# One wait of GpSimd for four tiles' results, and the first splits ahead of the first gates

## The chip, the cores and the metric

The kernel runs on one core of a Trainium2 chip. The metric is the device time of one execution in microseconds (us). The kernel is one program in which the five engines (TensorE or PE, VectorE or DVE, ScalarE or ACT, GpSimd or POOL, SyncE or SP) each follow an instruction list of their own and are tied together by semaphores alone.

## The reference

The input x is 16 images of 128 channels of 28 x 28 positions (784 tokens of an image). Three blocks follow one another, each added to its input:

```python
x = x + conv_block(group_norm(x))                 # depthwise 3x3, relu, prune, 1x1 conv, relu, prune
t = tokens(x)                                     # 16 x 784 tokens of 128 values
t = t + spiking_attention(layer_norm(t), Wq, Wk, Wv)
flat = layer_norm(t).reshape(12544, 128)
logits = flat @ Wr                                # 8 experts
top_vals, top_idx = top_k(logits, 2); w = softmax(top_vals)
for e in range(8):                                # every token: its two experts alone have a gate
    y = gelu(flat @ W1[e] + b1[e]) @ W2[e] + b2[e]   # 128 -> 512 -> 128
    out += gate[:, e] * y
t = t + out
```

The change touches the last block only, the experts.

## The kernel before, in words

**Stages.** The first 555 us work through the images (convolution, attention, norm, routing) as a software pipeline over images, one image entering in each step. Each routed image is sent by GpSimd to a dispatch buffer in DRAM ("dispatched_rows"), sorted by expert: 14 indirect transfers of 112 rows an image (L575). Images 14 and 15 are held back, and are normed, routed and sent between the first expert tiles. Then come 105 **expert tiles** of 256 dispatched rows with one expert each, and last the **sums**: for each of the 16 images the two expert rows of each token are loaded from DRAM, added (L1561), turned by TensorE (L891), added to the residual (L1567) and stored.

**One expert tile t**, by engine:
- SyncE loads its rows turned (`xrt`, four buffers, L438) and their fields (destination, the two experts' gate arguments, L441). The fields are handled in batches of four tiles (DEEP = 4).
- TensorE: `hidden(t)`, 12 matmuls of 256 columns (four parts of the hidden layer by three products of 16-bit halves, L839, pair_b or pair_c by the parity of t); `output(t)`, two halves of one bias matmul (L853) and 12 matmuls (L856) into pair_d. Its order is hidden(0), hidden(1), then for each t: hidden(t + 2), output(t).
- ScalarE: `gelu(t)` (L1041) and `high_half(t)`, the rounding to 16 bit (L1048), two instructions each, two tiles ahead; once for each batch `gate_tanh` (L1052).
- VectorE: `gated(t)` (L1520) multiplies pair_d by the gates' shares into `y`, a ring of 16 tiles, and raises the semaphore y_copied; then `split(t + 2)` (L1504), the low half of gelu, two instructions. Once for each batch, two tiles ahead of it, `fields` (L1495 to L1498: which expert is this tile's, tanh's argument, destination rows), which waits for the stores of the batch four earlier, and `gate` (L1512), which makes the shares.
- GpSimd: `store_tile(t)` waits for y_copied to reach t + 1 and issues two indirect transfers (L585, 128 rows of 512 bytes each) from y to "expert_rows" in DRAM. At tiles 9 to 15 and 21 to 27 it also issues the rows of images 14 and 15, two transfers ahead of each store of a tile (L575).

**What sets the order.** Each engine's order is written out by hand; there is no planner. GpSimd's DMAs go to a queue of their own (software_dynamic), SyncE's and ScalarE's to two others. After its last tile load SyncE issues the loads of the sums: images 0 to 5 when the stores of the first 88 tiles have landed, 6 to 12 when all hidden matmuls are done, 13 to 15 when all stores have landed (L483 to L485). The dispatched rows of images 14 and 15 are asked for at tile 72 (EARLY) by SyncE.

**Before the tile loop** ScalarE runs gelu(0), high_half(0), gate_tanh(0), gelu(1), high_half(1); VectorE runs fields(0), split(0), gate(0), split(1).

The lines that matter:

```python
def store_tile(t):                                   # GpSimd
    place, slot = t // DEEP % STORE_BATCHES, t % DEEP
    gate("y_copied", t + 1)
    for s in range(2):
        pool.indirect_dma_start(ys, ...dest[:, place, slot, s:s + 1]..., y[:, t % STORE_DEEP, s, :], ...)
```

Of the kernel before, what the change touches and what calls it, by code (L numbers as in the profile page):

```python
# [53 lines left out]
TILES = (2 * TOKENS + E * (TILE - 1)) // TILE  # L54
# [6 lines left out]
DEEP = 4  # L61
# [12 lines left out]
LATE_TABLES_AT = 26  # L74
LATE_PARTS = 6
PADS_AT = 44
POOL_CONSTS, FIRST_CONSTS = 31, 5
W_LOADS = 16
GELU_HALF = FC // 2
# [18 lines left out]
def build(nc, a, out):  # L98
# [7 lines left out]
    with ExitStack() as ctx:  # L106
# [155 lines left out]
        def some(value):  # L262


            return not (isinstance(value, int) and value <= 0)
# [21 lines left out]
        def held_step(i):  # L287

            return Step(i + 4, (i + 4) // 2, i % 2, held=True)
# [23 lines left out]
        def batch_of(t):  # L313

            return t // DEEP, t // DEEP % 2
# [14 lines left out]
        def _(sp):  # L330
# [112 lines left out]
            def place_pad(e):  # L443
                if e == 0:
                    sp.wait_ge(S["tables_late"], 1)
                place = table(mybir.EngineType.SP, pad_at, e, 1, XROWS - TILE)[0]
                sp.dma_start(xs[bass.ds(place, TILE), :].rearrange("(s p) c -> p s c", p=P), pad_rows[:, :, :].bitcast(U32)).then_inc(S["padded"], 16)
# [16 lines left out]
            for t in range(AHEAD, TILES):  # L464
                if PADS_AT <= t < PADS_AT + E:
                    place_pad(t - PADS_AT)
                if t == EARLY:
# [21 lines left out]
        def _(pool):  # L489
# [55 lines left out]
            def gate(name, value):  # L545


                pool.wait_ge(S[name], value)
                pool.sem_inc(S["gates"], 1)
# [30 lines left out]

            def store_tile(t):
                place, slot = t // DEEP % STORE_BATCHES, t % DEEP
                gate("y_copied", t + 1)
                for s in range(2):
                    pool.indirect_dma_start(  # L585
                        ys, bass.IndirectOffsetOnAxis(ap=dest[:, place, slot, s:s + 1].bitcast(U32), axis=0),
                        y[:, t % STORE_DEEP, s, :], None, bounds_check=table_end, oob_is_err=False).then_inc(S[f"stored_{place}"], 16)

            for t in range(TILES):
                for i in range(HELD, IMAGES):  # L590
                    at = HELD_AT[i - HELD] + 8
                    if t == at:
                        rows_whole(i)
                    if at < t <= at + NT:
                        send_rows(i % 2, t - at - 1)
                store_tile(t)
# [302 lines left out]
        def _(act):  # L899
# [45 lines left out]
            def norm_rows(out_, pair, n0, ts, done, width=P):  # L945
                for t in ts:
                    last = A.activation(out_[:, t, 0:width], pair[0:TT, t * P:t * P + width], ACT.Identity,
                                        scale=rstd[0:TT, n0 + t:n0 + t + 1], bias=shift[0:TT, n0 + t:n0 + t + 1])
                if NT - 1 in ts:
                    last.then_inc(S[done], 1)  # L950
# [22 lines left out]
            def high_rows(i, j, u):  # L973
                if some(16 * 2 * NT * j):
                    act.wait_ge(S[f"sent_{u}"], 16 * 2 * NT * j)
                act.wait_ge(S["xn2_ready"], i + 1)
                A.activation(rows[:, u, :, 0:P], xf[:, :, :], ACT.Identity).then_inc(S["hi_ready"], 1)
# [8 lines left out]
            def deviations(step):  # L986

                act.wait_ge(S["var_ready"], step.k + 1)
                A.activation(root[:, :], var[:, :], ACT.Sqrt).then_inc(S["root_ready"], 1)
# [41 lines left out]
            def half_of(tensor, t, h):  # L1031
                return tensor[:, t % 2, GELU_HALF * h:GELU_HALF * (h + 1), :].rearrange("p f k -> p (f k)")

            def gelu(t):
                hp = (pb, pc)[t % 2]
                if some(2 * (t - 1)):
                    act.wait_ge(S["ghl_ready"], 2 * (t - 1))
                for h in range(2):

                    act.wait_ge(S["h_ready"], 2 * t + h + 1)  # L1040
                    A.activation(half_of(g, t, h), hp[:, h * BANK:(h + 1) * BANK], ACT.Gelu, scale=1.0 / WSCALE).then_inc(S["g_ready"], 1)  # L1041

            def high_half(t):
                if some(t - 1):
                    act.wait_ge(S["y_ready"], t - 1)
                for h in range(2):
                    act.wait_ge(S["g_ready"], 2 * t + h + 1)
                    A.activation(ghl[:, t % 2, 0, h * 2 * TILE:(h + 1) * 2 * TILE], half_of(g, t, h), ACT.Copy).then_inc(S["g_hi_ready"], 1)  # L1048

            def gate_tanh(q, half):  # L1050
                act.wait_ge(S["arg_ready"], q + 1)
                A.activation(tanh[:, half, :, :], arg[:, half, :, :], ACT.Tanh).then_inc(S["tanh_ready"], 1)  # L1052

            gelu(0)
            high_half(0)
            gate_tanh(0, 0)
            gelu(1)
            high_half(1)
            for t in range(TILES):
                for i in range(HELD, IMAGES):  # L1060
                    at = HELD_AT[i - HELD]
                    if t == at + 2:
                        deviations(held_step(i))
                    if t == at + 4:
                        act.wait_ge(S["norm_ready"], i + 5)
                        act.wait_ge(S["lo_ready"], i)
                    if at + 4 <= t < at + 8:
                        norm_rows(xf, pa, NT, range(2 * (t - at - 4), min(2 * (t - at - 3), NT)), "xn2_ready", P - 1)
                    if t == at + 8:
                        high_rows(i, i // 2, i % 2)  # L1070
                if t + 2 < TILES:
                    gelu(t + 2)
                    high_half(t + 2)
                if t % DEEP == 2 and t + 2 < TILES:
                    q, half = batch_of(t + 2)
                    gate_tanh(q, half)
# [10 lines left out]
        def _(dve):  # L1087
# [16 lines left out]
            def bc_last(ap, n):  # L1104

                return ap.rearrange("p (t k) -> p t k", k=1).broadcast_to([ap.shape[0], ap.shape[1], n])
# [377 lines left out]
            def fields(q, half):  # L1484

                f = fld[:, half, :, :, :]
                first = q * DEEP
                place, uses = q % STORE_BATCHES, q // STORE_BATCHES
                if some(uses):
                    dve.wait_ge(S[f"stored_{place}"], 32 * DEEP * uses)  # L1490
                count = min(DEEP, TILES - q * DEEP)
                dve.wait_ge(S[f"fields_{half}"], 8 * DEEP * (q - half) + 16 * count)
                f = f[:, 0:count]
                link = Chain("dve_b", q)
                link(V.tensor_tensor(mine[:, half, 0:count, :], f[:, :, :, 1], bc_last(tile_expert[:, first:first + count], 2), ALU.is_equal))  # L1495
                V.scalar_tensor_tensor(out=arg[:, half, 0:count, :], in0=mine[:, half, 0:count, :], scalar=0.5, in1=f[:, :, :, 2],
                                       op0=ALU.subtract, op1=ALU.mult).then_inc(S["arg_ready"], 1)
                V.tensor_tensor(dest[:, place, 0:count, :], mine[:, half, 0:count, :], f[:, :, :, 0], ALU.add).then_inc(S["dest_ready"], 1)  # L1498

            def split(t):  # L1500

                for h in range(2):
                    dve.wait_ge(S["g_hi_ready"], 2 * t + h + 1)
                    V.tensor_tensor(ghl[:, t % 2, 1, h * 2 * TILE:(h + 1) * 2 * TILE], gv(t, h),  # L1504
                                    ghl[:, t % 2, 0, h * 2 * TILE:(h + 1) * 2 * TILE], ALU.subtract).then_inc(S["ghl_ready"], 1)

            def gv(t, h):
                return g[:, t % 2, 2 * h:2 * h + 2, :].rearrange("p f k -> p (f k)")

            def gate(q, half):  # L1510
                dve.wait_ge(S["tanh_ready"], q + 1)
                V.tensor_scalar(share[:, half, :, :], tanh[:, half, :, :], 0.5 / WSCALE, 0.5 / WSCALE, ALU.mult, ALU.add).then_inc(S["gate_ready"], 1)  # L1512

            def gated(t):
                slot, (q, half) = t % DEEP, batch_of(t)
                dve.wait_ge(S["y_ready"], t + 1)
                if slot == 0:
# [2 lines left out]
                V.tensor_tensor(y[:, t % STORE_DEEP, :, :], pd[:, b0:b0 + 2 * P].rearrange("p (s c) -> p s c", s=2),  # L1520
                                bc_last(share[:, half, slot, :], P), ALU.mult).then_inc(S["y_copied"], 1)

            fields(0, 0)
            split(0)
            gate(0, 0)
            split(1)
            for t in range(TILES):
                for i in range(HELD, IMAGES):
                    at, step = HELD_AT[i - HELD], held_step(i)
# [71 lines left out]
```

## Time and profile before

| | us |
|---|---|
| median of 3 runs | 1048.2 (1040.11 to 1049.55) |
| profiled execution, its own time | 1046.94 |
| its span, first to last instruction | 1045.1 |
| busy: PE / DVE / ACT / POOL | 740.7 / 564.6 / 494.0 / 462.7 |
| stores of the tiles (L585), 210 transfers | 213.8 busy |
| first and last result of a tile (L1520) | 562.4 and 994.8 |

How to read the rows further down. Times are us from the span's start unless marked ns. PE is the matmul side of TensorE, PEld its weight loads; the two overlap, and ends of matmuls are modelled. PEclk is the clock that TensorE was granted as a share of 2.4 GHz: 1.00 is 2.4 GHz, 0.50 is 1.2 GHz. A releaser in square brackets is what ended an engine's idle time; "issue" means that nothing in the profile explains it, "remote" that the semaphore came from something the profile doesn't show. L12 is line 12 of the kernel. A timeline row merges neighbours of one kind, with their number (x12). In a row of windows the busy times stand in the order PE, PEld, DVE, ACT, POOL, each with its number of instructions, then PEclk, the share of the DMA engines' time in use, and GB/s. A row of one line's instructions gives ns min/median/max, and the first and last start.

### The profile page before, as it was taken

Reading aid. Unit: us, or ns where it says so; the run is one execution under the profiler, and the core shown is the slowest. Engines: PE = TensorE matmul, PEld = TensorE weight load, DVE = VectorE, ACT = ScalarE, POOL = GpSimd, SP = SyncE. Lnnn points to the kernel's source line nnn. Section 1 sums busy time; section 2 is a strip of 40 time slices with the busy share of each in tenths; the row PEclk is TensorE's granted clock in tenths of the full one; section 3 lists DMA queues with packets and bytes.
Section 4 is the critical chain, followed back from the end, with each engine's and each line's share of the span. In section 5 each row is a group of like instructions: output and inputs, shape, how many; then the busy total and the mean of one; then the engine's idle time right before and its main releaser. Section 6 shows DMA issues by size and latency. Waiting matters only on the chain.

```text
span 1045.1 us, 20792 instructions
## 1 busy us (share of the span) xinstructions
PE 740.7 (71%) x6748; PEld 530.1 (51%) x6748; DVE 564.6 (54%) x1756; ACT 494.0 (47%) x955; POOL 462.7 (44%) x488
## 2 busy tenths in 40 slices
PE   2777667766667568666657857858888887988754
PEld 1444334423444235433436735637767776777643
DVE  5678456544565457444654624426544544454477
ACT  2367336543455336443536715525655655565500
POOL 5000554345533553445443465556555555555510
PEclk9899788876886678767868968969999999999955
DMA  6654344322442233322123322323443333432897
GB/s 175 181 150 149 68 122 119 116 82 78 127 118 85 74 122 113 103 83 65 58 58 77 65 58 58 66 55 75 91 92 77 71 72 71 70 72 64 200 310 270
DMA packets 137297, 108.71 MB, mean 104 GB/s; under 512 B 98451, under 2 KB 119447, under 8 KB 137202
## 3 DMA queue, kind: packets, MB, share of 16 engines
q1 hardware_dynamic: 119570, 75.00, 28.8%
q0 software_dynamic: 13888, 26.03, 8.8%
q10 hardware_dynamic: 3744, 6.43, 1.7%
q8 instruction: 58, 0.95, 0.4%
q14 instruction: 37, 0.30, 0.1%
HBM read 45.26 MB, written 42.85 MB: 84 GB/s over the span
## 4 chain that ended last, share of the span: by engine, by line
PE 48%; issue 21%; ACT 9%; DVE 9%; another core or an unknown queue 7%; DMA 4%; SPq 1%; POOL 1%; DVEq 0%; ACTq 0%; POOLq 0%
PE pair_d L856 12%; PE pair_a L648 8%; PE pair_b L839 6%; PE pair_c L839 5%; PE pair_c L734 3%; DMA out<-seen_g 2%; ACT xb_x L1048 2%; PE pair_c L704 2%; PE pair_d L662 2%; ACT seen_g L966 2%; PE pair_c L724 1%; PE pair_a L683 1%; ACT seen_g L1041 1%; DMA conv_planes<-conv_y 1%
## 5 line engine op out<-in xcount | busy, mean ns | idle before, releaser
L585 POOL DMA_INDIRECT expert_rows<-conv_y,dest x210 | 213.8, 1018 | 196.9 <-DVE conv_y L1520 150.9
L575 POOL DMA_INDIRECT dispatched_rows<-p_area,pos x224 | 212.7, 949 | 187.9 <-DVE p_area L1320 110.8
L856 PE MATMUL pair_d<-w,xb_x 128*128 x2520 | 197.1, 226 | 41.4 <-issue 40.7
L856 PEld LDWEIGHTS pair_d<-w,xb_x 128*128 128x128 f16 x2520 | 166.1, 101 | 56.9 <-issue 51.0
L1048 ACT ACTIVATE xb_x<-seen_g 128x512 f16<-128x512 f32 x210 | 120.6, 625 | 154.8 <-remote 136.6
L648 PE MATMUL pair_a<-conv_y,p_area 128*32 128x392 f16 x1152 | 109.8, 442 | 85.4 <-issue 75.9
L1504 DVE TENSOR_TENSOR xb_x<-seen_g,xb_x 128x512 f16<-128x512 f32 x210 | 135.8, 688 | 28.2 <-ACT xb_x L1048 22.2
L1520 DVE TENSOR_TENSOR conv_y<-pair_d,share 128x256 f32<-128x256 f32 x105 | 44.3, 422 | 195.8 <-remote 170.5
L648 PEld LDWEIGHTS pair_a<-conv_y,p_area 128*32 128x32 f16 x1152 | 39.8, 114 | 138.0 <-issue 120.4
L839 PE MATMUL pair_c<-xrt,w 128*128 128x256 f16 x624 | 89.0, 283 | 26.0 <-issue 25.6
L839 PE MATMUL pair_b<-xrt,w 128*128 128x256 f16 x636 | 87.7, 288 | 10.6 <-issue 8.4
L559 POOL TENSOR_TENSOR conv_y<-conv_y 128x784 f16<-128x784 f32 x16 | 26.3, 1643 | 150.4 <-ACT conv_y L926 150.4
L966 ACT ACTIVATE seen_g<-pair_c 112x672 bf16<-112x672 f32 (+1 forms) x64 | 30.1, 471 | 127.4 <-remote 114.6
L839 PEld LDWEIGHTS pair_c<-xrt,w 128*128 x624 | 59.6, 101 | 42.4 <-issue 35.8
L1041 ACT ACTIVATE seen_g<-pair_b 128x512 f32<-128x512 f32 x106 | 58.7, 592 | 35.6 <-remote 32.1
L839 PEld LDWEIGHTS pair_b<-xrt,w 128*128 x636 | 63.2, 104 | 23.0 <-issue 14.1
L1257 DVE TENSOR_TENSOR seen_g<-seen_g,causal 112x784 bf16<-112x784 bf16 x16 | 9.1, 569 | 97.9 <-ACT seen_g L966 95.6
L966 ACT ACTIVATE seen_g<-pair_a 112x784 bf16<-112x784 f32 (+2 forms) x48 | 30.6, 637 | 64.2 <-remote 31.2
L1041 ACT ACTIVATE seen_g<-pair_c 128x512 f32<-128x512 f32 x104 | 56.0, 588 | 6.3 <-remote 5.0
L853 PE MATMUL pair_d<-b,two_rows 128*128 x210 | 47.5, 226 | 9.5 <-issue 4.7
L724 PE MATMUL pair_a<-p_area 128*112 128x512 bf16 (+3 forms) x80 | 22.1, 342 | 38.9 <-issue 31.0
L1264 DVE TENSOR_TENSOR p_area<-pair_c,xb_x 128x784 f32<-128x784 f32 x16 | 25.7, 1608 | 41.3 <-PE pair_c L734 30.8
(241 smaller groups left out, 1162.3 us busy)
## 6 DMA issues: line engine op xcount, KB each, us to landing
conv_y<-conv_planes SPq DMA_DIRECT2D x64, 225.0 KB
xb_x<-in_x SPq DMA_DIRECT2D x32, 392.0 KB, 4.1
p_area<-expert_rows SPq DMA_DIRECT2D x12, 784.0 KB
conv_planes<-conv_y SPq DMA_DIRECT2D x32, 225.0 KB
t_all<-p_area SPq DMA_DIRECT2D x16, 392.0 KB, 3.0
out<-seen_g ACTq DMA_DIRECT2D x16, 392.0 KB, 7.9
t_all<-in_L_ffn_W SPq DMA_DIRECT2D x16, 256.0 KB, 5.0
dispatched_rows<-p_area,pos POOLq DMA_INDIRECT x224
```

The lines of the kernel that those rows point to most:

```text
L575: pool.indirect_dma_start(xs, bass.IndirectOffsetOnAxis(ap=pos[:, u, t, k:k + 1].bitcast(U32), axis=0), rows[:, u, t, :].bitcast(U32), Non ...
L585: pool.indirect_dma_start(ys, bass.IndirectOffsetOnAxis(ap=dest[:, place, slot, s:s + 1].bitcast(U32), axis=0), y[:, t % STORE_DEEP, s, :] ...
L648: last = T.matmul(pa[g * GROUP_CHANNELS:(g + 1) * GROUP_CHANNELS, h * BANK:h * BANK + HALF], tap_w[:, g, tap, :], stacked_rows[:, u, g, ky ...
L724: last = T.matmul(score_pair(t)[0:TT, c0:c1], sk[:, t * TT:(t + 1) * TT], sq[:, t * TT + c0:t * TT + c1], start=True, stop=True)
L839: last = T.matmul(hp[:, f * TILE:(f + 1) * TILE], w1[:, wp, bass.ds(w0 + f * P, P)], xrt[:, slot, xp, :], start=(m == 0), stop=(m == 2))
L853: T.matmul(dst, two_rows[:], b2[:, bass.ds(c0, P)], start=True, stop=False)
L856: last = T.matmul(dst, ghl[:, t % 2, gp, f * TILE + s * P:f * TILE + (s + 1) * P], w2[:, wp, bass.ds(w0 + f * P, P)], start=False, stop=(f ...
L966: A.activation(seen[:, t * L + t * TT:(t + 1) * L], score_pair(t)[0:TT, 0:L - t * TT], ACT.Sign).then_inc(S["seen_ready"], 1)
L1041: A.activation(half_of(g, t, h), hp[:, h * BANK:(h + 1) * BANK], ACT.Gelu, scale=1.0 / WSCALE).then_inc(S["g_ready"], 1)
L1048: A.activation(ghl[:, t % 2, 0, h * 2 * TILE:(h + 1) * 2 * TILE], half_of(g, t, h), ACT.Copy).then_inc(S["g_hi_ready"], 1)
L1504: V.tensor_tensor(ghl[:, t % 2, 1, h * 2 * TILE:(h + 1) * 2 * TILE], gv(t, h), ghl[:, t % 2, 0, h * 2 * TILE:(h + 1) * 2 * TILE], ALU.subt ...
L1520: V.tensor_tensor(y[:, t % STORE_DEEP, :, :], pd[:, b0:b0 + 2 * P].rearrange("p (s c) -> p s c", s=2), bc_last(share[:, half, slot, :], P) ...
```

## The change

From tile 24 on (SINGLY) GpSimd waits at the first tile of each batch of four for the results of the whole batch, and not at the other three; the transfers and their order stay. Tile 104 is the last batch, alone. Ahead of the tile loop ScalarE does tile 0's gate_tanh behind gelu and high_half of tile 1, and VectorE does both splits ahead of fields(0) and gate(0).

```diff
+SINGLY = 6 * DEEP
...
             def store_tile(t):
                 place, slot = t // DEEP % STORE_BATCHES, t % DEEP
-                gate("y_copied", t + 1)
+                if t < SINGLY:
+                    gate("y_copied", t + 1)
+                elif slot == 0:
+                    gate("y_copied", min(t + DEEP, TILES))
                 for s in range(2):
                     pool.indirect_dma_start(
...
             gelu(0)
             high_half(0)
-            gate_tanh(0, 0)
             gelu(1)
             high_half(1)
+            gate_tanh(0, 0)
             for t in range(TILES):
...
+            split(0)
+            split(1)
             fields(0, 0)
-            split(0)
             gate(0, 0)
-            split(1)
             for t in range(TILES):
```

## Rows read from the trace of the kernel before

**Rows 1.** The page: busy time of each engine, and the chain that ended last.

```profile
PE 740.7 (71%) x6748; PEld 530.1 (51%) x6748; DVE 564.6 (54%) x1756; ACT 494.0 (47%) x955; POOL 462.7 (44%) x488
...
PE 48%; issue 21%; ACT 9%; DVE 9%; another core or an unknown queue 7%; DMA 4%; SPq 1%; POOL 1%; DVEq 0%; ACTq 0%; POOLq 0%
```

**Rows 2.** Windows, tile 28's result to tile 104's: busy us (instructions), PEclk, DMA share.

```profile
713.70:994.80 281.10, 235.89 (x2847) 204.02 (x2845) 138.60 (x313) 158.18 (x317) 151.52 (x152) 0.98 0.43 88
```

**Rows 3.** Groups of instructions, the same stretch: the stores alone.

```profile
L585 POOL DMA_INDIRECT expert_rows<-conv_y,dest x152 | 152.0, 1000 | 130.7 <-DVE conv_y L1520 98.7 <-issue 31.9
```

**Rows 4.** Waits, the same stretch: us in total, times, longest.

```profile
POOL expert_rows L585 <- DVE conv_y L1520: 98.7, 62, 3.6
...
PE pair_d L856 <- issue: 19.6, 31, 1.2
...
PE pair_c L839 <- issue: 13.1, 22, 1.2
...
PE pair_b L839 <- issue: 7.8, 13, 1.1
```

**Rows 5.** Timeline, the first matmuls of two tiles in turn: start, us, engine, line.

```profile
903.67 1.47 PE L839 MATMUL pair_b<-xrt,w 128*128 128x256 f16 x12
...
906.43 1.47 PE L839 MATMUL pair_c<-xrt,w 128*128 128x256 f16 x12
```

**Rows 6.** Timeline, a run of four stores and PE beside it.

```profile
909.70 0.98 POOL L585 DMA_INDIRECT expert_rows<-conv_y,dest  x1 [1.82 <-DVE conv_y L1520]
...
913.80 0.55 PE L856 MATMUL pair_d<-w,xb_x 128*128 x7
...
915.50 0.45 PE L856 MATMUL pair_d<-w,xb_x 128*128 x5 [1.15 <-issue]
```

**Rows 7.** Windows: a run of eight GpSimd transfers, and what follows it.

```profile
691.80:697.80 6.00, 6.00 (x59) 4.96 (x56) 4.05 (x12) 3.17 (x6) 4.78 (x5) 0.73 0.40 88
697.80:703.30 5.50, 1.07 (x9) 0.69 (x7) 0.00 (x0) 0.00 (x0) 3.10 (x4) 0.87 0.17 46
706.00:708.00 2.00, 2.00 (x12) 1.43 (x10) 1.93 (x5) 1.36 (x3) 1.70 (x2) 0.50 0.29 73
708.00:710.00 2.00, 2.00 (x30) 1.98 (x29) 1.86 (x8) 0.60 (x1) 1.70 (x2) 0.84 0.23 52
```

**Rows 8.** One line's instructions, 690 to 704: the eight transfers of that run.

```profile
L585 POOL DMA_INDIRECT expert_rows<-conv_y,dest x4: 976/977/982, 691.8 to 698.3; - x4
...
L575 POOL DMA_INDIRECT dispatched_rows<-p_area,pos x4: 945/950/1168, 694.3 to 700.9; - x4
```

**Rows 9.** Timeline: first matmuls of a tile, with PEclk at 0.50.

```profile
692.47 2.71 PE L839 MATMUL pair_b<-xrt,w 128*128 128x256 f16 x12
```

**Rows 10.** Windows: a run of fourteen in the stage ahead of the experts, 440 to 458.5.

```profile
440.00:451.00 11.00, 8.04 (x71) 4.80 (x70) 7.04 (x36) 4.30 (x9) 8.56 (x9) 0.76 0.31 86
451.00:458.50 7.50, 2.91 (x13) 0.51 (x5) 0.00 (x0) 0.00 (x0) 4.89 (x6) 0.50 0.16 47
```

**Rows 11.** Timeline, the first tiles: DVE and ACT.

```profile
555.46 0.17 DVE L1495 TENSOR_TENSOR mine<-fld,tile_expert 128x8 f32<-128x8 f32 x1 [9.61 <-DMA fld<-dispatched_rows]
...
557.31 1.29 DVE L1504 TENSOR_TENSOR xb_x<-seen_g,xb_x 128x512 f16<-128x512 f32 x2 [1.41 <-ACT xb_x L1048]
...
559.78 1.10 ACT L1041 ACTIVATE seen_g<-pair_b 128x512 f32<-128x512 f32 x2
...
562.43 0.42 DVE L1520 TENSOR_TENSOR conv_y<-pair_d,share 128x256 f32<-128x256 f32 x1 [1.71 <-PE pair_d L856]
```

**Rows 12.** Timeline, the last tiles, and the transfers behind them.

```profile
991.12 0.42 DVE L1520 TENSOR_TENSOR conv_y<-pair_d,share 128x256 f32<-128x256 f32 x1
...
997.37 1.70 POOL L585 DMA_INDIRECT expert_rows<-conv_y,dest  x1 [0.30 <-issue]
...
1007.89 4.83 SPq L455 DMA_DIRECT2D w<-expert_rows  x2
```

**Rows 13.** Windows, the stretch of the sums.

```profile
1005.00:1015.00 10.00, 4.62 (x21) 3.67 (x21) 6.68 (x6) 0.00 (x0) 0.00 (x0) 0.50 1.01 354
```

## The prediction

> **What bounds the kernel now.** I read the chain that ended last first: TensorE holds 48% of it and "issue" 21%, GpSimd 1% [rows 1]. "Issue" is time in which an engine waited for nothing the profile shows, so the next question is where TensorE has it and who is busy then. The expert tiles are the place. From tile 28's result to tile 104's, 281.1 us for 76 tiles or 14.8 us for four, TensorE is busy 235.9 us, GpSimd 151.5, VectorE 138.6, ScalarE 158.2 [rows 2]. GpSimd is no bound of its own there: its 152 stores take 152.0 us, and it idles 98.7 us for VectorE's results [rows 3, 4]. TensorE's missing time is mostly three waits put down to "issue", 19.6 + 13.1 + 7.8 = 40.5 us, or 2.1 us for each four tiles [rows 4]. Without them a tile passes in 906.43 - 903.67 = 2.76 us [rows 5].
>
> The timeline says when they come. GpSimd starts four stores in a row at 909.70; TensorE goes on at full pace, breaks off in the middle of a group at 913.80 + 0.55 = 914.35 and goes on at 915.50 [rows 6]: the stall begins 4.65 us into the run of stores and lasts until shortly after it. A longer run makes it plain. Eight transfers, four stores and four row sends of image 15, lie back to back from 691.8 to 700.9 + 0.95 = 701.85 [rows 8]. TensorE is busy all of the first 6.0 us and then 1.07 us of the next 5.5; VectorE and ScalarE are at 0.00, with nothing to work on [rows 7]. In the stage ahead of the experts GpSimd sends fourteen transfers that wait for no tile, and TensorE, then busy with convolutions, falls to 2.91 us in 7.5 [rows 10]. So it is not TensorE's lateness that makes the run long; the run starves TensorE's instruction stream after some 4 us, and until about 1.4 us after its end (703.3 - 701.85).
>
> **The change part by part.** *The waits.* Of tiles 24 to 104, 81 waits become 21 (tiles 24, 28, ..., 104). The 60 that go cost nothing now, since GpSimd idles behind them [rows 3], and give nothing.
>
> *The stores, bunched.* Work and number stay; the pattern changes. Eight stores then lie back to back behind every fourth tile, where now runs of four (5 us) alternate with pauses. Queued behind the new wait are only stores and, for tiles 25 to 27, image 15's row sends. VectorE waits for stores four batches back before it writes a batch's destinations, 11 tiles or some 40 us later: that covers the stores' new lateness of up to 11 us.
> - Stall of one run of eight. Lower end, the measured run: 5.5 - 1.07 = 4.4 us lost [rows 7]. There TensorE came in partly at the low clock (0.73) and so reached the starved point late. Upper end: the starved point at 4.65 us as in [rows 6], the end at 10.1 + 1.4 = 11.5, so 6.9 us at the same lost share (4.4/5.5 = 0.8), 5.5 us. I take 4.7, nearer to the only measured run of eight. Less the 2.1 us now paid: +2.6 us for four tiles.
> - The clock. In this stage it is granted at 0.98 [rows 2]. Behind the run of eight it stood at 0.50, the 1.2 GHz level, still from 706 to 708, and came back in 708 to 710 at a mean of 0.84, so at about 708.6 [rows 7]; TensorE had been all but idle for 5.5 us before. At the low level the first twelve matmuls of a tile take 2.71 us against 1.47 [rows 5, 9]. The 5.3 us from 703.3 to 708.6 then cost 5.3 x (1 - 1.47/2.71) = 2.4 us. Bounds: 0 (the clock holds, as behind the runs of four) and 2.4. I take 1.6, two thirds, as one row can't say that every run brings the fall.
> - Sum for a group: 2.6 + 1.6 = 4.2 us; the runs behind tiles 27, 31, ..., 99 fall on 19 groups: +80 us.
>
> The Trainium skill speaks against this reading: "SBUF — State Buffer", section "Who interferes with whom", says that a DMA never contends with a compute engine and that TensorE and ScalarE never wait on anyone. By that page the group's +4.2 us would be 0. The trace doesn't agree where TensorE loses 4.4 of 5.5 us [rows 7], although that page speaks of memory ports and not of instruction supply.
>
> *The first batch.* Tiles 24 to 27 lose today's run of eight (-4.4 - 1.6), and the run that follows them has fourteen transfers, eight stores and six sends: 14 x 1.27 + 1.4 - 4.65 = 14.5 us at 0.8 is 11.6, against 4.7 in the sum above, +6.9. Together +1.
>
> *The tail.* Tile 103's result starts at 991.12, so its run goes from some 991.8 to 1002.0, and tile 104's two stores to 1004.5; now the last ends at 997.37 + 1.70 = 999.07 [rows 12]. The loads of the last images are issued behind those stores, the last two now from 1007.89 on, and so come up to 5.5 us later. In between the transfer engines are full (share 1.01) [rows 13] with other images, which hides part; against that, the transposes run starved too. Bounds 0 and 8, I take +3.
>
> *The first splits and gelu.* ScalarE no longer does tile 0's tanh between its two tiles: at most 0.2 us earlier. VectorE's first split ran at 557.31, 1.4 us after the batch's gates begun at 555.46; it waited for ScalarE and not for the fields, so nothing is gained [rows 11]. What is late next: arg comes behind the second split, at some 561.0; ScalarE's tanh, and behind it gelu of tile 2, now at 559.78, move to about 561.3. Gelu 2 is then done at 562.4, and its high half waits for tile 0's output, ready at 562.43, anyway. The gates are there by 561.9, ahead of that same product. Bounds -0.2 and +0.6, I take 0.
>
> **Sum.** 80 + 1 + 3 + 0 = 84 us. The profiled execution took 1046.94 us (span 1045.1), so 1131; the median of the three runs, 1048.2, is 1.3 above it, within their spread. Forecast: **1131 us**. Its own range: with 4.4 us and no clock loss 19 x 2.3 = 44, so 1090; with 5.5 and 2.4, 19 x 5.8 = 110 and a tail of 8, so 1165.
>
> **The rivals.**
> - *A, nothing moves.* TensorE's loss goes by how much GpSimd transfers in all, not by how it is bunched, or is not GpSimd's doing. For it: the page above; and three of four transfers stay what they are. Against it: twelve full-pace matmuls right beside a run's first transfers, and none beside its last [rows 6, 7]. Time: 1047 + 3 of the tail, 1050.
> - *B, faster.* Each run costs TensorE one stall of fixed size, the 1.15 us of [rows 6], wherever it stands in the run; half as many runs then halve the 40.5 us: 1047 - 20 + 3 = 1030. It decides if the stall behind a run of eight is under 2.1 us. For it: the stalls behind runs of four look alike. Against it: 4.4 us behind eight [rows 7], and the fourteen [rows 10].
> - *C, a milder loss.* After the longer pause, some 7 us instead of 2, TensorE enters the run with more instructions in hand and starves later, at 7 to 8 us into it: about 3.5 us x 0.8 = 2.8 to 3.2 lost, +1 us a group, clock unchanged: 1047 + 19 + 4 = 1070. For it: the fourteen, where the first 11 us still brought 8.04 us of work [rows 10], though with other matmuls.
> - That the change doesn't do what it says can be left aside: the first wait of a batch asks for its last tile, bounded by the number of tiles, and tile 104 stands alone.
>
> **Chances.** Forecast 0.62, A 0.14, B 0.12, C 0.12. Within 1% of 1048.2 us, about what a measurement of this kernel can tell from no change, lies A. Faster is B; slower are the forecast and C: 0.12, 0.14, 0.74. The range has to take in A and C from below and the forecast's top, and leaves out B: 1044 to 1165.
>
> **What would show it.** In the profile after: GpSimd's stores in runs of eight with its wait for VectorE once for four tiles (bunching right); TensorE's "issue" waits in the tiles' stage at some 19 x 4.7 = 89 us instead of 40.5, each cluster from about 4.65 us into a run to 1.4 us behind it (starving right); PEclk in that stage below 0.9 (clock right); four tiles in about 19 us instead of 14.8. If the clusters end 1.2 us after they begin, B holds. If they stay as they are, A. If PEclk stays at 0.98, the 1.6 us a group are wrong. The last two loads of expert rows should be issued at some 5 us more behind the last tile's result than the 13.1 us now (1007.89 - 994.8).

## The result, and the profile after

The changed kernel takes 1138.9 us (median of 4 runs, 1127.39 to 1139.92) against 1048.3 of the kernel before: ratio 1.086, 95% interval 1.081 to 1.090, 91 us slower. The forecast was 1131. The profiled execution took 1139.65 us with a span of 1137.9, 92.8 longer than before.

In this kernel's numbering the results are L1524, the stores L589, TensorE's output L860 and hidden layer L843. First the page, busy time and the chain that ended last, to be held against [rows 1]:

```profile
PE 789.4 (69%) x6748; PEld 553.1 (49%) x6748; DVE 569.0 (50%) x1756; ACT 499.3 (44%) x955; POOL 462.2 (41%) x488
...
PE 52%; issue 23%; ACT 7%; another core or an unknown queue 6%; DVE 6%; DMA 4%; SPq 1%; POOL 0%; DVEq 0%; ACTq 0%; POOLq 0%
```

The same 6748 matmuls are busy 48.7 us longer, GpSimd's work is what it was, and GpSimd, with 1% of the chain before, is at 0%.

Windows: tile 24's result to tile 28's, and then tile 28's to tile 104's in two parts with a cut at tile 32's. Columns as in [rows 2].

```profile
690.80:704.30 13.50, 13.32 (x159) 12.32 (x157) 11.33 (x33) 10.58 (x21) 1.63 (x2) 0.88 0.26 46
704.30:737.30 33.00, 18.50 (x169) 14.28 (x168) 10.99 (x28) 6.81 (x15) 18.05 (x19) 0.74 0.21 52
737.30:1089.10 351.80, 266.79 (x2681) 216.56 (x2681) 130.96 (x287) 154.42 (x300) 136.27 (x139) 0.79 0.31 72
sum 384.80, PE 285.29 PEld 230.84 DVE 141.95 ACT 161.23 POOL 154.32; mean PE 142.64 PEld 115.42 DVE 70.97 ACT 80.62 POOL 77.16
```

The 76 tiles that took 281.1 us [rows 2] now take 384.8: +103.7, more than the whole loss. Before them tiles 24 to 27 gained 9.7 us (13.5 against 23.2), and what follows the last result is 1.5 us shorter. PEclk has fallen from 0.98 to 0.79.

Waits from 704.3 to 1089.1, us in total, times and longest, to be held against [rows 4]: GpSimd's largest in the first fence, TensorE's in the second.

```profile
POOL expert_rows L589 <- DVE conv_y L1524: 176.7, 18, 10.6
```

```profile
PE pair_d L860 <- issue: 66.8, 98, 1.8
PE pair_b L843 <- issue: 25.4, 41, 1.2
```

TensorE waits 92.2 us for nothing the profile shows, against 40.5; GpSimd waits 18 times where it waited 62 times.

One group in the timeline: the first and last stores of a run of eight, TensorE between them, and VectorE's results:

```profile
950.42 0.98 POOL L589 DMA_INDIRECT expert_rows<-conv_y,dest  x1 [10.33 <-DVE conv_y L1524]
...
951.09 0.83 PE L860 MATMUL pair_d<-w,xb_x 128*128 x12
...
954.54 0.47 PE L860 MATMUL pair_d<-w,xb_x 128*128 x4
...
955.47 0.22 PE L860 MATMUL pair_d<-w,xb_x 128*128 x1 [0.47 <-issue]
...
956.19 0.42 DVE L1524 TENSOR_TENSOR conv_y<-pair_d,share 128x256 f32<-128x256 f32 x1 [4.79 <-remote]
...
956.21 0.33 PE L860 MATMUL pair_d<-w,xb_x 128*128 x3 [0.52 <-issue]
...
956.90 0.26 PE L860 MATMUL pair_d<-w,xb_x 128*128 x1 [0.37 <-issue]
...
957.64 0.38 PE L860 MATMUL pair_d<-w,xb_x 128*128 x2 [0.48 <-issue]
...
959.37 0.97 POOL L589 DMA_INDIRECT expert_rows<-conv_y,dest  x1 [0.30 <-issue]
...
961.91 1.86 PE L843 MATMUL pair_b<-xrt,w 128*128 128x256 f16 x8 [0.62 <-issue]
```

TensorE runs on until 954.54 + 0.47 = 955.01, 4.6 us into the run, then gets one to three matmuls at a time, and goes on at 961.91, 1.6 us after the run's end (960.34). This is one run; a mean over all 18 runs of eight, from the trace's matmul records, begins less sharply: TensorE works all of the first three us of a run, 0.75 of the fourth, 0.42 of the fifth and about 0.3 of each from there to the end. The windows of that stall, and of the clock behind it:

```profile
955.00:961.90 6.90, 2.47 (x13) 1.03 (x12) 1.72 (x3) 1.75 (x3) 4.13 (x5) 0.64 0.14 48
961.90:966.00 4.10, 4.09 (x31) 3.56 (x31) 1.72 (x3) 2.61 (x5) 0.00 (x0) 0.50 0.27 48
966.00:970.90 4.90, 4.90 (x58) 4.44 (x56) 2.92 (x8) 3.46 (x8) 0.00 (x0) 0.89 0.26 46
```

### The profile page after: what moved, and what is told of

Its sections match the earlier page's. It is cut to its first block, busy times and chain, and to the rows that moved or that the text cites. A ratio compares the mean times of both kernels' runs of the same rounds, so it can differ in the third digit from the quotient of the medians.

```text
span 1137.9 us, 20732 instructions
## 1 busy us (share of the span) xinstructions
PE 789.4 (69%) x6748; PEld 553.1 (49%) x6748; DVE 569.0 (50%) x1756; ACT 499.3 (44%) x955; POOL 462.2 (41%) x488
## 3 DMA queue, kind: packets, MB, share of 16 engines
q0 software_dynamic: 13888, 26.03, 7.6%
## 4 chain that ended last, share of the span: by engine, by line
PE 52%; issue 23%; ACT 7%; another core or an unknown queue 6%; DVE 6%; DMA 4%; SPq 1%; POOL 0%; DVEq 0%; ACTq 0%; POOLq 0%
PE pair_d L860 14%; PE pair_a L652 8%; PE pair_b L843 7%; PE pair_c L843 5%; PE pair_c L738 3%; DMA out<-seen_g 2%; PE pair_c L728 2%; PE pair_b L687 2%; PE pair_d L666 2%; ACT seen_g L970 2%; PE pair_d L751 1%; PE pair_c L708 1%; ACT xb_x L1052 1%; DMA conv_planes<-conv_y 1%
## 5 line engine op out<-in xcount | busy, mean ns | idle before, releaser
L589 POOL DMA_INDIRECT expert_rows<-conv_y,dest x210 | 212.0, 1010 | 303.1 <-DVE conv_y L1524 235.8
L860 PE MATMUL pair_d<-w,xb_x 128*128 x2520 | 218.2, 238 | 89.3 <-issue 84.8
L860 PEld LDWEIGHTS pair_d<-w,xb_x 128*128 128x128 f16 x2520 | 179.6, 107 | 108.6 <-issue 104.3
L1524 DVE TENSOR_TENSOR conv_y<-pair_d,share 128x256 f32<-128x256 f32 x105 | 44.5, 424 | 283.1 <-remote 215.4
L652 PE MATMUL pair_a<-conv_y,p_area 128*32 128x392 f16 x1152 | 117.5, 453 | 86.1 <-issue 77.5
L843 PE MATMUL pair_b<-xrt,w 128*128 128x256 f16 x636 | 109.6, 321 | 29.8 <-issue 26.2
L843 PE MATMUL pair_c<-xrt,w 128*128 128x256 f16 x624 | 86.8, 289 | 14.3 <-issue 14.2
L843 PEld LDWEIGHTS pair_b<-xrt,w 128*128 x636 | 66.2, 110 | 62.8 <-issue 50.7
L1045 ACT ACTIVATE seen_g<-pair_c 128x512 f32<-128x512 f32 x104 | 58.4, 593 | 65.7 <-remote 64.6
L843 PEld LDWEIGHTS pair_c<-xrt,w 128*128 x624 | 62.6, 104 | 28.6 <-issue 20.0
L857 PE MATMUL pair_d<-b,two_rows 128*128 x210 | 50.1, 239 | 6.4 <-issue 4.1
```

Source lines behind the costliest of these rows:

```text
L589: pool.indirect_dma_start(ys, bass.IndirectOffsetOnAxis(ap=dest[:, place, slot, s:s + 1].bitcast(U32), axis=0), y[:, t % STORE_DEEP, s, :] ...
L652: last = T.matmul(pa[g * GROUP_CHANNELS:(g + 1) * GROUP_CHANNELS, h * BANK:h * BANK + HALF], tap_w[:, g, tap, :], stacked_rows[:, u, g, ky ...
L843: last = T.matmul(hp[:, f * TILE:(f + 1) * TILE], w1[:, wp, bass.ds(w0 + f * P, P)], xrt[:, slot, xp, :], start=(m == 0), stop=(m == 2))
L857: T.matmul(dst, two_rows[:], b2[:, bass.ds(c0, P)], start=True, stop=False)
L860: last = T.matmul(dst, ghl[:, t % 2, gp, f * TILE + s * P:f * TILE + (s + 1) * P], w2[:, wp, bass.ds(w0 + f * P, P)], start=False, stop=(f ...
```

## The experiments

Two theories stood first. R: a run of GpSimd transfers that lie back to back starves TensorE from some 4.6 us into it until 1.5 us behind it, and the clock falls with the idle engine. W: what costs is GpSimd's waiting for several tiles at once, the lateness of the stores. Each run has its own comparison with the kernel before on the same chip; all ratios are to that.

### Each part alone

batch_only is the changed kernel with the three moved lines of the first batch (gate_tanh and two splits) put back; splits_only is the kernel before with only those moved.

> The kernel after without its second part: tile 0's gates stand again ahead of the second gelu and between the two splits. Theory R (runs of GpSimd transfers starve TensorE's instructions; the second part is worth nothing): 1138 us, within 1% of the kernel after, groups of four tiles at 20.2 us. Rival S (the moved splits share in the loss, by a late gelu that throws the tiles' order off): clearly under 1138, by 10 us or more.

> The kernel before with the second part alone. Theory R: 1048 us, within 1% of the kernel before; first result of a tile within 1 us of 562.4. Rival S: slower by 10 us or more.

Measured: batch_only 1140.7 us, ratio 1.087 (1.083 to 1.091); splits_only 1049.8 us, 0.999 (0.996 to 1.002). The whole loss is the batched wait. The moved lines are worth nothing that can be measured, as the working of the prediction had it.

### Other lengths of the batch

```diff
-                elif slot == 0:
-                    gate("y_copied", min(t + DEEP, TILES))
+                elif t % 2 == 0:                              # batch2; batch8: 8 in both places
+                    gate("y_copied", min(t + 2, TILES))
```

> The kernel after, but from tile 24 on GpSimd waits at every second tile for the results of two tiles. Theory R: the runs are of four transfers again, as those that arise by themselves before; 1048 us within 1.5%, four tiles in about 14.8 us, PEclk near 1. Rival W (it is the waiting for a later tile than the one stored, or the missing waits, that costs, whatever the length of the run): half of the loss stays, some 1090 us.

> The kernel after, but with one wait for eight tiles (tiles 24 to 103: ten batches) and so runs of sixteen transfers. Theory R, sized by the trace of after: TensorE works through some 3.9 us worth of tiles at the start of a run, a sixth of its pace until 1.4 us after the end, and full pace from then on but for one fall of the clock: 20.4 + 1.4 us, then 22.1 - 3.9 - 3.0 = 15.2 us of work left plus 2 for the clock, 39 us for eight tiles against 2 x 20.25 = 40.5 of after: 1138 - 15 = about 1125, with issue waits of TensorE as large as after's. Rival B (each run costs a fixed stall): the loss over before halves once more, some 1095 us. Rival P (the loss grows with the length of the run without end): over 1138.

Measured: batch2 1072.0 us, ratio 1.022 (1.018 to 1.026); batch8 1154.5 us, 1.100 (1.095 to 1.104). Windows of batch2, tile 28's result to tile 104's, and of batch8, eight batches of eight tiles:

```profile
712.40:1020.70 308.30, 244.18 (x2856) 206.48 (x2854) 140.52 (x312) 158.44 (x315) 157.52 (x154) 0.98 0.38 83
```

```profile
753.90:1090.90 337.00, 225.22 (x2434) 183.30 (x2432) 116.37 (x256) 139.87 (x272) 124.79 (x128) 0.77 0.27 58
```

In batch2 four tiles take 16.2 us instead of 14.8, between what R and W said: neither is right there. The 27.2 us over 76 tiles are TensorE's (with the small ones of the bias matmul counted too, its "issue" waits are 39.3 + 12.1 + 9.4 = 60.8 us against 19.6 + 13.1 + 7.8 + 1.7 = 42.2, and it is busy 8.3 longer), with PEclk at 0.98. All its stores lie in runs of four, 38 of them, where the kernel before has 28 to 30 (by how short a pause ends a run) and the others in shorter ones; at some 1.45 us a run (42.2 / 29) the eight to ten more explain 12 to 15 of the 18.6 us of waits, an estimate, and the rest is not settled. In batch8 eight tiles take 42.1 us, 21.1 for four, behind runs of sixteen: more than with runs of eight (19.5). So a run doesn't cost a fixed amount (B's 1095 is refuted, and the time lies on P's side), and R's 1125 isn't right either: it had the clock recover better than 0.77 and the "issue" waits as large as after's, and they are 68.9 + 36.2 + 4.3 = 109.4 us over 64 tiles, 6.8 for four against 4.9.

### A pause between the transfers

If it is the lack of a pause that starves TensorE, a pause mends it with the waits left as they are. after_pause is the changed kernel with a GpSimd fill of 128 x 512 values behind each store from tile 24 on, 0.55 us, and a wait ahead of it for the fill before; before_pause has it behind each tile's two stores, with the single waits; after_tick fills only 128 x 16. (The wait is shortened to a comment here.)

```diff
+            def pause(words):
+                ...                                 # wait for the fill before this one
+                G.memset(spare_area[:, 0:words], 0.0).then_inc(S["paused"], 1)
...
                     pool.indirect_dma_start(ys, ...)
+                    if t >= SINGLY:
+                        pause(512)                  # after_tick: 16
```

> The kernel after with a memset of 128x512 16-bit values in the chip memory (some 0.5 us of GpSimd's own work, no transfer) behind each store from tile 24 on: the same waits and bunches, but no two transfers back to back, and GpSimd busy for some 15 us behind every fourth tile instead of 10. Theory R (it is transfers back to back that starve TensorE): the pauses let instructions in and the loss shrinks: under 1138, down to some 1060 where four tiles take 15.5 us. Rival G (any work of GpSimd starves, or a pause of 0.5 us is too short to let instructions in): the starved time grows with the 15 us, four tiles in 23 to 24 us, about 1200.

> The kernel before with the same memset of some 0.5 us behind each tile's two stores, all 105 tiles, so that no more than two transfers lie back to back. Theory R: the clusters of issue waits at the end of runs of four shrink, 1048 - 10 to - 20. Rival G: GpSimd works 105 x 0.5 = 52 us more within the same stage, its unbroken stretches of four tiles' work grow from 5.1 to 6.1 us, and the time rises by 10 to 30 us.

> The changed kernel with a fill of 128 x 16 values behind each store from tile 24 on, instead of 128 x 512 (0.55 us). Theory K (any instruction of GpSimd's that is no transfer, and the wait ahead of it, breaks the run): as after_pause, 1021 us or up to 10 less. Theory R (time without a transfer is what TensorE needs): the fill takes 0.1 us or less, most of the loss stays, 1090 to 1140 us.

Measured: after_pause **1021.4 us**, ratio 0.973 (0.969 to 0.978), 117 us less than the same kernel without the fills; before_pause 1044.2, 0.996 (0.993 to 1.000), with tiles 28 to 104 as long as before (281.9 us); after_tick 1146.7, 1.092 (1.089 to 1.096). Of R's figures none was met: after_pause gained more than its 1060 at best, after_tick lies 7 us above its range, and before_pause brought 4 us instead of 10 to 20: its "issue" waits over the 76 tiles are still 22.7 + 9.5 + 4.2 + 2.7 = 39.1 us against 42.2. Windows of after_pause, tile 28's result to tile 104's, and TensorE's largest wait there:

```profile
706.00:964.60 258.60, 231.97 (x2847) 200.32 (x2845) 140.24 (x312) 159.26 (x313) 231.81 (x295) 0.99 0.46 95
```

```profile
PE pair_d L871 <- issue: 15.2, 41, 0.5
```

Four tiles now take 13.6 us, the three "issue" waits come to 15.2 + 2.8 + 2.6 = 20.6 us (92.2 without the fills, 40.5 in the kernel before), GpSimd is busy for 231.8 of the 258.6 us, and PEclk is 0.99. Its timeline (first fence) and after_tick's (second):

```profile
906.14 0.97 POOL L598 DMA_INDIRECT expert_rows<-conv_y,dest  x1 [0.17 <-issue]
...
907.10 0.55 POOL L589 MEMSET spare_area<- 128x512 f16 x1
...
907.81 0.97 POOL L598 DMA_INDIRECT expert_rows<-conv_y,dest  x1 [0.16 <-issue]
```

```profile
995.99 0.98 POOL L598 DMA_INDIRECT expert_rows<-conv_y,dest  x1 [10.24 <-DVE conv_y L1535]
996.96 0.13 POOL L589 MEMSET spare_area<- 128x16 f16 x1
997.27 0.97 POOL L598 DMA_INDIRECT expert_rows<-conv_y,dest  x1 [0.18 <-issue]
```

The short fill disappears in the gap of 0.30 us that lies between two transfers anyway: they start 1.28 us apart, as without it. The long one moves them to 1.67 us apart. One other instruction between two transfers does nothing; the time does. TensorE beside after_tick's run, 5.0 us into it and then the next 5.5:

```profile
996.00:1001.00 5.00, 4.07 (x56) 3.47 (x53) 0.96 (x3) 0.88 (x2) 4.37 (x8) 1.00 0.31 70
1001.00:1006.50 5.50, 1.34 (x10) 0.79 (x11) 1.72 (x3) 1.75 (x3) 4.39 (x8) 0.86 0.14 48
```

That VectorE, ScalarE or the buffers are late because of the batched wait is refuted by after_pause: the wait is there, and the kernel is faster than the one before.

### Transfers that move nothing

hollow8 puts eight more transfers behind each bunch of the changed kernel, whose row numbers all lie out of bounds, so that they are issued and move no row.

```diff
+                if t >= SINGLY and slot == DEEP - 1:
+                    for n in range(8):
+                        pool.indirect_dma_start(ys, ...far_rows[:, 0:1]..., y[:, t % STORE_DEEP, 0, :], ...)
```

> The kernel after with eight more indirect transfers behind each bunch of stores from tile 24 on, all of whose row numbers lie beyond the bound, so that they are issued and move nothing. GpSimd has the time: it idles 10.3 us of the 20.25. Theory D (what starves is GpSimd's issuing of transfers): runs of sixteen in four tiles, 20.4 + 1.4 us starved and some 6 behind, 28 us for four tiles, about 1290. Rival M (what starves is the moving of the rows): as after, 1138 to 1150.

Measured: 1344.6 us, ratio 1.279 (1.273 to 1.286), +206 on the changed kernel, and 55 above theory D's estimate: four tiles take 30.9 us and not 28. A real and a hollow transfer in its timeline, and the windows of one run of sixteen:

```profile
1028.57 1.02 POOL L591 DMA_INDIRECT expert_rows<-conv_y,dest  x1 [0.30 <-issue]
1029.90 0.98 POOL L596 DMA_INDIRECT expert_rows<-conv_y,far_rows  x1 [0.30 <-issue]
```

```profile
1019.50:1040.00 20.50, 8.60 (x75) 5.35 (x73) 2.79 (x6) 3.33 (x7) 15.69 (x16) 0.67 0.18 40
```

A hollow transfer takes GpSimd as long as a real one, and starves TensorE as well: 8.6 us of work in 20.5. Issuing is what costs, not the rows that move. (A hollow transfer isn't quite without traffic: GpSimd's queue has 19008 packets against 13888, or 32 small ones for each, but 26.12 MB against 26.03. The making of the transfers and these packets aren't told apart.) "Perfetto Trace Analysis" in the Trainium skill, section "DMA Instruction — SWDGE (GPSIMD)", says that the end shown for such an instruction is when its descriptors are made and not when the data has moved; the equal 0.98 us agree.

### The same remedy where the kernel before suffered too

[rows 10] showed the stall in the stage ahead of the experts. sends_pause is the kernel before, expert tiles untouched, with a fill of 128 x 1024 values (0.97 us) behind each pair of row sends of images 0 to 13; sends_half has 128 x 512.

```diff
-            def send_rows(u, t):
+            def send_rows(u, t, i=None):
                 for k in range(2):
                     pool.indirect_dma_start(...)
+                if i is not None:                    # images 0 to 13
+                    ...                              # wait for the fill before this one
+                    G.memset(spare_area[:], 0.0).then_inc(S["paused"], 1)
```

> The kernel before with a memset of 128x1024 16-bit values (some 0.95 us of GpSimd) behind each pair of row sends in the stage ahead of the tiles: seven pairs an image, 14 images. Theory R: no run of fourteen there, TensorE's crawl by the end of each image's sends shrinks, and the 555 us stage gets shorter by 2 to 5 us an image: 990 to 1025. Rival G: GpSimd's stretch of work grows from 17.8 to 25 us an image, the crawl with it: slower, 1060 to 1130.

> The kernel before, with the fill of sends_pause behind each pair of row sends cut from 128 x 1024 to 128 x 512 values of 16 bits (0.55 us instead of 0.97). Theory R (TensorE starves only where transfers leave no pause; 0.55 us was enough behind every single store in after_pause, where here two transfers lie between pauses): GpSimd, which is now itself in the chain, gets 98 x 0.42 = 41 us back where it is the bound, so 905 to 941 us. Theory L (it is the share of GpSimd's time left free that counts, 0.97 of 2.9 us in sends_pause, 0.55 of 2.5 us here against 0.55 of 1.5 in after_pause): only part of the relief, 960 to 1010 us.

Measured: sends_pause **941.4 us**, ratio 0.896 (0.891 to 0.901), 107 us less than before and more than R had said; sends_half 999.2, 0.953 (0.948 to 0.958), in the range of theory L. TensorE's largest wait from 300 to 540 us in the kernel before, and the windows from 300 to 450, before and in sends_pause, whose image stage ends there:

```profile
PE pair_a L648 <- issue: 37.0, 38, 2.3
```

```profile
300.00:450.00 150.00, 99.97 (x732) 59.12 (x734) 83.46 (x339) 71.26 (x135) 67.42 (x68) 0.77 0.35 105
```

```profile
300.00:450.00 150.00, 112.20 (x877) 73.29 (x878) 107.08 (x376) 89.93 (x173) 130.31 (x131) 0.86 0.40 107
```

From 300 to 447 us TensorE's "issue" waits come to 22.3 + 16.0 + 4.2 + 3.6 = 46.1 us in the kernel before and to 0.9 + 0.7 + 0.2 = 1.8 in sends_pause: there the stall is gone.

The first expert tile's result comes at 447.1 us instead of 562.4, in sends_half at 515.0. Where GpSimd waited 110.8 us in all for VectorE's rows, it now waits 0.3. The page of sends_pause, the chain that ended last:

```profile
PE 33%; POOL 22%; issue 17%; DVE 9%; DMA 6%; ACT 5%; another core or an unknown queue 5%; SPq 2%; POOLq 0%; DVEq 0%; ACTq 0%
```

GpSimd is in the chain with 22%, 13% for its row sends and 7% for the fills: in the image stage the remedy is now part of what bounds, and it still pays. With the shorter fill GpSimd waits for VectorE's rows again (98.9 us in all), so only part of the starving is gone: behind pairs 0.55 us is too little, as it was in before_pause.

The mean distance from start to start sorts these runs as well as the pause does: 1.25 to 1.28 us without fills (full stall), 2.90 / 2 = 1.45 in sends_half and 2.95 / 2 = 1.48 in before_pause (partly or hardly relieved), 1.67 in after_pause and 3.52 / 2 = 1.76 in sends_pause (little or no stall left). Whether TensorE needs a long enough pause or a slow enough pace of transfers isn't told apart by any run here.

### Both together

pauses_single is the kernel before with sends_pause's and before_pause's fills; pauses_batched the changed kernel with sends_pause's and after_pause's.

> The kernel before with both pauses: 0.97 us behind each pair of row sends (sends_pause, 941.4) and 0.55 us behind each tile's two stores (before_pause, 4 us less than before). If the two are independent, 941.4 - 4 = 937 us (930 to 943). If the expert stage behind the earlier start is another one, it moves by more.

> The changed kernel with both pauses: 0.97 us behind each pair of row sends and 0.55 us behind each store from tile 24 on. If independent, 941.4 - (1047.9 - 1021.4) = 915 us (908 to 925). If the gain of after_pause came from the batched wait rather than from pauses behind single stores, this is also below pauses_single by 22 us; otherwise the two differ by what a pause behind every store and not every second brings.

Measured: pauses_single 933.3 us, ratio 0.890 (0.886 to 0.893); pauses_batched **910.9 us**, 0.868 (0.866 to 0.871), the fastest kernel of the study, 137 to 139 us below the kernel before. Both lie within 4 us of the sum of their parts (937 and 915), so the gains add up. That the batched one leads by 22 us doesn't show that the batched wait helps: it has a fill behind every store, the single one behind every second, and the two were not crossed.

```profile
595.40:847.20 251.80, 224.70 (x2731) 194.20 (x2732) 134.04 (x298) 155.63 (x307) 223.46 (x289) 0.98 0.41 85
```

These are its windows from tile 28's result to tile 100's: 72 tiles, 14.0 us for four, with GpSimd busy 89% of the time.

## Why the prediction was right

**Bunching, starving, clock** all showed as named. The stall shown lasts from 4.6 us into the run (4.65 forecast) until 1.6 us behind it (1.4). The "issue" waits come to 92.2 us where 89 were forecast. That closeness is partly luck: the 92.2 hold the group with the run of fourteen. The 18 groups behind it, tile 32's result to tile 104's, show the plain runs of eight; TensorE's largest wait there in the changed kernel, and then in the kernel before with the windows:

```profile
PE pair_d L860 <- issue: 53.2, 82, 1.1
```

```profile
PE pair_d L856 <- issue: 17.7, 28, 1.2
```

```profile
726.90:994.80 267.90, 223.92 (x2700) 193.56 (x2699) 127.58 (x287) 149.36 (x300) 144.40 (x145) 0.98 0.43 89
```

With pair_b and pair_c these waits are 53.2 + 25.4 = 78.6 us, 4.4 a run where I took 4.7, against 17.7 + 13.1 + 7.8 = 38.6, so +2.2 us a group and not +2.6.

**The clock term was too small.** Over the same 76 tiles, 2849 matmuls against 2847, TensorE is busy 285.3 - 235.9 = 49.4 us longer, 2.6 us a group; over the 18 plain groups it is 266.8 - 223.9 = 42.9, or 2.4. I took 1.6 and had 2.4 as the upper bound. The step that was mis-sized is "the 5.3 us from 703.3 to 708.6": it counted only the work behind the stall. The windows from 955.0 on show 0.64 already within the stall, so that the matmuls that trickle through it take longer too, and 0.50 or a mean of 0.89 for the nine us behind it. Over the stretch a PEclk of 0.79 is (1 - 0.79) / 0.5 x 384.8 = 162 us at the low level, 8.5 a group. My two thirds, for runs that leave the clock alone, had no ground either: the trace's clock record has a stretch at the low level for every one of the 19 runs, 6.8 to 10.2 us long behind the runs of eight, and each of these begins before the stall is over. Not all of the 49.4 us is the clock, though: a lone matmul takes 0.22 us at the full level (955.47), one in a row of twelve 0.83 / 12 = 0.07. Sorting the matmul records by level gives some 43 us for the clock and the rest for such broken rows, an estimate. Waits and slower matmuls make 51.7 + 49.4 = 101.1 of the 103.7 us.

**Where the 84 us stood, and where the 92.8 lie.** In the kernel before, tiles 32 to 104 took 267.9 us, now 351.8: 83.9 over 18 groups, 4.7 each (4.2 forecast, 76 over 18). The group with the run of fourteen took 33.0 instead of 13.2: +19.8, where 4.2 + 6.9 = 11.1 were forecast. Its "issue" waits grew by (66.8 - 53.2) - (19.6 - 17.7) = 11.7 us against 2.6 + 6.9 = 9.5, and TensorE is busy 18.5 - 12.0 = 6.5 longer, where its extra term had nothing for the clock, which stands at 0.74 there. Against that, tiles 24 to 27 gained 9.7 and not 6.0: GpSimd has 2 transfers in that stretch where it had 14, so besides the run of eight shorter ones went too. The tail, forecast at +3, came to -1.5. The last loads of expert rows are issued 1109.0 - 1089.1 = 19.9 us behind the last result (13.1 before), so about 7 later, near the 5 expected, and what follows the last result is no longer for it, with the transfer engines full:

```profile
1100.00:1110.00 10.00, 4.50 (x21) 3.52 (x21) 5.34 (x5) 0.00 (x0) 2.52 (x3) 0.50 1.02 338
```

The DMA engines were full before the change [rows 13] and are full now. The start was worth nothing, as forecast (first result at 562.2, was 562.4; splits_only 0.999). 83.9 + 19.8 - 9.7 - 1.5, and 0.3 ahead of tile 24, are the 92.8. So 1131 is as near as it is in part by luck. In each plain group the stall was taken 0.4 us too long and the clock 0.8 too short; and the 7.9 us missing in the 18 groups and the 8.7 in the group of the fourteen are offset by 3.7 at tiles 24 to 27 and 4.5 at the tail.

**The rivals.** A (nothing moves) and B (a fixed stall) fall with 1.086; B's claim that half the runs halve the loss falls with batch8 too. C, an onset at 7 to 8 us after a longer pause, is refuted by the onset at 4.6 us behind 10.33 us of GpSimd's idling. The Trainium skill's rule in "SBUF — State Buffer", section "Who interferes with whom", by which A would have held, speaks of memory ports; taken beyond ports, the runs disagree with its sentence that a DMA never contends with a compute engine (8.6 us of TensorE's work in 20.5 in hollow8).

**What stays open.** Why issuing starves TensorE isn't shown: no view has a record of where its instructions are held. It gets on in steps of about 0.7 us within a stall (955.47, 956.21, 956.90, 957.64). A late loading of code isn't the plain answer: in 14 of the 18 stalls behind runs of eight no packet of the queues of kind "instruction" is under way, and around the one shown the nearest come at 952.8 and 965.1. Pause and pace aren't told apart (above). Idling in another form than a fill, and fill lengths between 0.13 and 0.55 us behind single stores, weren't tried.

## What to carry to other kernels

Where "issue" waits of one engine cluster behind a row of GpSimd's indirect transfers that lie back to back, look at the length of the row before looking at the engine. Don't bunch such transfers; where many are due at once, put some useful GpSimd work between them, or even a fill. Here 0.55 us behind each single one did it, or 0.97 us behind each pair; longer fills weren't tried. A stall is to be priced together with the clock that it takes down, within the stall and behind it.

## What the runs showed of the hardware

- Transfers issued by GpSimd 1.28 us apart leave TensorE 1.3 us of work in 5.5 from some 5 us on; 1.67 us apart they leave 20.6 us of unexplained waits over 76 tiles (92.2 at 1.28 us) and a clock of 0.99. A fill of 0.13 us behind each changes neither the distance nor the stall.
- It is the issuing, not the rows: transfers that move no row take the same 0.98 us and cost 206 us in hollow8.
- GpSimd time spent on nothing can be the best bargain in a kernel: 98 x 0.97 = 95 us of fills on GpSimd bring the first result of the experts 115 us earlier.
- The granted clock follows the stalls: 0.98 with runs of four, 0.79 with runs of eight, each over the 76 tiles; one fall for each of the 19 runs.
